# Projections split into chunks and a woven instruction order in a one-core Mamba, attention and feed-forward kernel

## What is computed

```
x = x + layernorm(mamba(layernorm(x)))
x = x + layernorm(two_layers(layernorm(x)))

mamba:   xb, z = split(x @ in_proj);  xb = silu(conv4(xb) + conv_b)
         dt = softplus(...); state = exp(dt * a) * state + dt * b * xb; y = sum(state * c)
         out = ((y + D * xb) * silu(z)) @ out_proj
layer:   q, k, v = split(shift(x) @ wqkv); q, k normalised and rotated; o = local_attention(q, k, v)
         x = x + o @ wo
         a, g = split(layernorm(shift(x)) @ w1 + b1);  x = x + (a * gelu(g)) @ w2 + b2
```

## Time and profile before

| | |
|---|---|
| time, median of 3 runs | 2461.28 us (2460.6 to 2464.99) |
| time of the profiled execution | 2461.61 us |
| its span, first to last instruction | 2459.8 us |
| mean granted clock of TensorE | 0.943 of full speed |
| instructions | 44075 |

### The profile page before, as it was taken

One profiled execution on the slowest core, in us unless ns is written; L12 is line 12 of the kernel. 1 busy time (PEld: TensorE's weight loads), 2 busy tenths in 40 slices (PEclk: granted clock), 3 DMA queues, 4 the chain that ended last, 5 costly groups with the idle time before them and its releaser, 6 DMA issues.

```text
span 2459.8 us, 44075 instructions
## 1 busy us (share of the span) xinstructions
PE 1893.9 (77%) x15808; PEld 1114.3 (45%) x15936; DVE 1892.7 (77%) x3477; ACT 1778.1 (72%) x3955; POOL 1711.4 (70%) x1540
## 2 busy tenths in 40 slices
PE   2156778797878879797878879697888879787865
PEld 0013345353635445363635445363645545363634
DVE  3557797978879797988878797988879797887442
ACT  2245778696978878696878878696877869685644
POOL 1969595977959596886959596885959597792010
PEclk9977999899999989999999999999999989999988
DMA  4444443535344343534544353534543353531000
GB/s 162 126 120 115 112 105 104 132 83 146 103 130 117 100 121 92 134 86 131 129 129 103 103 124 96 138 87 130 130 115 99 110 127 90 137 99 33 17 20 9
DMA packets 126346, 261.09 MB, mean 106 GB/s; under 512 B 26928, under 2 KB 59696, under 8 KB 125872
## 3 DMA queue, kind: packets, MB, share of 16 engines
q1 hardware_dynamic: 126128, 258.27, 39.6%
HBM read 185.42 MB, written 42.99 MB: 93 GB/s over the span
## 4 chain that ended last, share of the span: by engine, by line
PE 38%; DVE 23%; ACT 13%; issue 9%; POOL 8%; DMA 4%; SPq 0%; DVEq 0%; POOLq 0%; ACTq 0%
DVE hs L618 6%; DVE m L892 4%; PE f_bank L342 4%; PE b_bank L342 4%; DVE kr L906 3%; POOL gy L663 3%; DMA spread<-steps 3%; POOL dbu L646 3%; ACT da L594 3%; PE b_bank L703 3%; PE f_bank L746 3%; PE y_sum L571 2%; DVE b_bank L896 2%; PE b_bank L773 2%; DVE ss L879 2%
## 5 line engine op out<-in xcount | busy, mean ns | idle before, releaser
L618 DVE TENSOR_TENSOR_SCAN hs<-da,dbu 128x512 f32<-128x512 f32 x512 | 622.2, 1215 | 127.1 <-POOL dbu L646 82.0
L663 POOL TENSOR_TENSOR gy<-hs,bc 128x512 f32<-128x512 f32 x512 | 652.1, 1274 | 41.5 <-DVE hs L618 31.2
L646 POOL TENSOR_TENSOR dbu<-spread,bc 128x512 f32<-128x512 f32 x512 | 651.5, 1274 | 9.1 <-DMA spread<-steps 9.0
L594 ACT ACTIVATE da<-spread,rest 128x512 f32<-128x512 f32 x512 | 359.4, 702 | 159.0 <-DVE hs L618 135.1
L703 PE MATMUL b_bank<-rest,h_t 128*128 128x512 f32 x384 | 227.9, 694 | 96.6 <-DVE kr L906 92.5
L960 POOL TENSOR_TENSOR kr<-kr,rn 128x512 f32<-128x512 f32 x256 | 264.8, 1043 | 42.3 <-ACT rn L817 37.0
L703 PE MATMUL f_bank<-rest,h_t 128*128 128x512 f32 x384 | 217.6, 665 | 72.1 <-DVE kr L906 64.2
L571 PE MATMUL y_sum<-gy,rest 128*32 128x512 f32 x1024 | 147.0, 649 | 92.4 <-POOL gy L663 92.3
L342 PE MATMUL f_bank<-first,kr 128*128 128x128 f32 x768 | 128.4, 298 | 78.9 <-DVE kr L906 49.8
L342 PE MATMUL b_bank<-first,kr 128*128 128x128 f32 x768 | 123.7, 296 | 57.8 <-DVE kr L906 41.8
L1106 POOL TENSOR_TENSOR xs<-xs,v 128x512 f32<-128x512 f32 x16 | 18.9, 1183 | 213.3 <-ACT xs L337 213.3
(11 more groups left out here) (168 smaller groups left out, 4748.2 us busy)
## 6 DMA issues: line engine op xcount, KB each, us to landing
spread<-steps SPq DMA_DIRECT2D x256, 512.0 KB, 5.1
vs<-v SPq DMA_DIRECT2D x96, 260.0 KB, 5.9
bc<-bc_rows SPq DMA_DIRECT2D x32, 512.0 KB, 6.2
steps<-k_t SPq DMA_DIRECT2D x32, 512.0 KB, 2.7
gate<-gates SPq DMA_DIRECT2D x32, 512.0 KB, 5.7
gates<-kr SPq DMA_DIRECT2D x16, 512.0 KB, 3.4
gates<-late SPq DMA_DIRECT2D x16, 512.0 KB, 4.3
vs<-v SPq DMA_DIRECT2D x32, 130.0 KB, 4.5
```

The source lines that it names most:

```text
L594: e.activation(da[:, :], spread[:, slot(b, s // 2), 0, :], ACT.Exp, scale=a_neg[:, s:s + 1]).then_inc(decayed.sem, 1)
L618: e.tensor_tensor_scan(hs[:, s % 2, :], da[:, :], dbu[:, s % 2, :], 0.0, ALU.mult, ALU.add).then_inc(scanned.sem, 1)
L646: e.tensor_tensor(dbu[:, s % 2, :], spread[:, slot(b, s // 2), 1, :], bc[:, s % 2, :], ALU.mult).then_inc(fed.sem, 1)
L663: e.tensor_tensor(gy[:, s % 8, :], hs[:, s % 2, :], bc[:, 2 + s % 2, :], ALU.mult).then_inc(read_out.sem, 1)
```

## The change

- **Chunks of wo.** The four turns of o and the wo projection become steps `turn_out(c)` and `project_out(c)`. Turns 0 and 1 go ahead of the last head's values (they need heads 0 to 3 only); the projection runs as one step for each chunk, four matmuls for the four token tiles, accumulating in X[1] instead of O. Turns 0, 2 and 3 go through X[0].
- **Chunks of w2 and of the output projection.** w2 runs as three steps, each behind the gate of its chunk, and the output projection as two. For B, w2 sums into L1 instead of L0 (`f.sum`), and what frees the banks for the next element's takes follows.
- **Tables.** In several ACT steps `use_table` goes ahead of the wait.
- **Weaving.** A letter's stream now runs through all elements; the word is repeated, and a second string says how many steps of each letter are left out at first, in place of `AHEAD`. The one-time table work moves into the first step of M.
- **New words for all five engines.** Most of the order is as before. For one period, with +0 for the element whose position the letter gives, PE and SP read as follows where they differ most:

```diff
-def weave(word, **streams):
+def weave(word, late, **chains):
-    for part in word.split():
-        for _ in range(int(part[1:]) if part[0] in streams else 0):
-            next(streams[part[0]], None)
-    for s in streams.values():
-        for _ in s:
-            pass
+    late = {part[0]: int(part[1:]) for part in late.split()}
+    while chains:
+        for part in word.split():
+            for _ in range(int(part[1:])):
+                if late[part[0]]:
+                    late[part[0]] -= 1
+                elif part[0] in chains and next(chains[part[0]], chains) is chains:
+                    del chains[part[0]]
...
+                self.sum = L0 if w is wf else L1
...
         def act_norm_scale(E, e, w, b):
+            E.use_table(EXP_LN)
             E.wait_ge(*w.measured(b, 1))
-            E.use_table(EXP_LN)
...
-            E.wait_ge(*gated(b, 1))
             E.wait_ge(*scanned(b, NSCAN - 1))
-            for t in range(NT):
-                for h in range(NH2):
-                    op = e.matmul(da[:, t * P:(t + 1) * P], yg[h][:, t * P:(t + 1) * P], w_out[:, h, :], start=h == 0,
-                                  stop=h == 1)
-            op.then_inc(out_projected.sem, 1)
-            yield
+            for h in range(NH2):
+                E.wait_ge(*gated(b, h))
+                for t in range(NT):
+                    op = e.matmul(da[:, t * P:(t + 1) * P], yg[h][:, t * P:(t + 1) * P], w_out[:, h, :],
+                                  start=h == 0 and t == 0, stop=h == 1, skip_group_check=True)
+                if h:
+                    op.then_inc(out_projected.sem, 1)
+                yield
...
-                    E.wait_ge(*(f.gelu_made(b - 1, 2), f.gated(b - 1, 2), f.added(b - 1))[n])
+                    E.wait_ge(*(f.added(b - 1) if bank is f.sum else f.gated(b - 1, 2)))
...
+            def turn_out(c):
+                E.wait_ge(*w.o_done(b, 2 * c + 1))
+                if c < 2:
+                    E.wait_ge(*w.p_copied(b, HEADS - 2 + c))
+                else:
+                    E.wait_ge(*w.o_copied(b, 0 if c == 2 else 2))
+                pe_turn(e, X[c == 1], lambda n: w.o[:, n, c * P:(c + 1) * P]).then_inc(w.o_turned.sem, 1)
+
+            def project_out(c):
+                E.wait_ge(*w.o_copied(b, c))
+                if c == 0:
+                    E.wait_ge(*w.o_copied(b, 1))
+                for t in range(NT):
+                    op = e.matmul(X[1][:, t * P:(t + 1) * P], w.o_t[:, c, t * P:(t + 1) * P], wo[:, l, c, :],
+                                  start=c == 0 and t == 0, stop=c == NC - 1, skip_group_check=True)
+                return op
...
+                else:
+                    for c in range(2):
+                        turn_out(c)
+                        yield
                 value(2 * g + 1)
                 yield
...
+            turn_out(2)
+            yield
+            for c in range(2):
+                project_out(c)
+                yield
+            turn_out(3)
+            yield
+            project_out(2)
+            yield
+            project_out(3).then_inc(w.wo_done.sem, 1)
             yield
...
-            E.wait_ge(*f.gated(b, 2))
-            for t in range(NT):
-                for c, (c0, n) in enumerate(HCH):
-                    k = P if c == 2 else n
-                    op = e.matmul(L0[:, t * P:(t + 1) * P], f.ff[0:k, c, t * P:(t + 1) * P], w2[0:k, l, c, :], start=c == 0,
-                                  stop=c == 2)
-            op.then_inc(f.out.sem, 1)
-            yield
+            for c, (c0, n) in enumerate(HCH):
+                k = P if c == 2 else n
+                if c == 0:
+                    E.wait_ge(*(f.gated(b, 1) if f is f0 else f.gelu_made(b, 2)))
+                E.wait_ge(*f.gated(b, c))
+                for t in range(NT):
+                    op = e.matmul(f.sum[:, t * P:(t + 1) * P], f.ff[0:k, c, t * P:(t + 1) * P], w2[0:k, l, c, :],
+                                  start=c == 0 and t == 0, stop=c == 2, skip_group_check=True)
+                if c == 2:
+                    op.then_inc(f.out.sem, 1)
+                yield
```

More of the change, by code:

```diff
@@ L587, in act_state @@
             else:
+                act_tables(E, e)
                 E.wait_ge(*a_made(0))
@@ L611, in skip @@
                                        ALU.add).then_inc(skipped.sem, 1)
+            if b == 0:
+                dve_tables(E, e)
             for s in range(NSCAN):
@@ L761, in pe_attention @@
                     yield
+                else:
+                    for c in range(2):
+                        turn_out(c)
+                        yield
                 value(2 * g + 1)
                 yield
-            E.wait_ge(*w.o_done(b, HEADS - 1))
-            for c in range(NC):
-                if c > 1:
-                    E.wait_ge(*w.o_copied(b, c - 2))
-                pe_turn(e, X[c % 2], lambda n: w.o[:, n, c * P:(c + 1) * P]).then_inc(w.o_turned.sem, 1)
-                yield
-            E.wait_ge(*w.o_copied(b, NC - 1))
-            for t in range(NT):
-                for c in range(NC):
-                    op = e.matmul(O[:, t * P:(t + 1) * P], w.o_t[:, c, t * P:(t + 1) * P], wo[:, l, c, :],
-                                  start=c == 0, stop=c == NC - 1)
-            op.then_inc(w.wo_done.sem, 1)
+            turn_out(2)
+            yield
+            for c in range(2):
+                project_out(c)
+                yield
+            turn_out(3)
[3 more added lines that the diff above has]
+            project_out(3).then_inc(w.wo_done.sem, 1)
             yield
@@ L869, in act_attention @@
                 E.wait_ge(*w.o_turned(b, c))
-                e.activation(w.o_t[:, c, :], X[c % 2][:, :], ACT.Copy).then_inc(w.o_copied.sem, 1)
+                e.activation(w.o_t[:, c, :], X[c == 1][:, :], ACT.Copy).then_inc(w.o_copied.sem, 1)
                 yield
@@ L944, in dve_attention @@
             E.wait_ge(*w.wo_done(b))
-            e.tensor_tensor(x[:, :, :], x[:, :, :], tm(O), ALU.add).then_inc(w.x_added.sem, 1)
+            e.tensor_tensor(x[:, :, :], x[:, :, :], tm(X[1]), ALU.add).then_inc(w.x_added.sem, 1)
             yield
@@ L1048, in dve_feed_forward @@
             E.wait_ge(*f.out(b))
-            e.tensor_tensor(x[:, :, :], x[:, :, :], tm(L0), ALU.add).then_inc(f.added.sem, 1)
+            e.tensor_tensor(x[:, :, :], x[:, :, :], tm(f.sum), ALU.add).then_inc(f.added.sem, 1)
             yield
@@ L1156, in act_tables, with program, elements @@
         def act_tables(E, e):
+            E.use_table(EXP_LN)
             E.wait_ge(*rest_loaded(0))
-            E.use_table(EXP_LN)
             e.activation(a_neg[:, :], a_neg[:, :], ACT.Exp).then_inc(a_exp.sem, 1)
-        def program(name, streams, once=None, at=0):
+        def program(name, **streams):
+            def elements(E, e, stream):
+                for b in range(B):
+                    yield from stream(E, e, b)
             def body(e):
                 E = Engine(e)
-                for k in range(-3, B + 1):
-                    if k == at and once:
-                        once(E, e)
-                    weave(ORDER[name], **{letter: stream(E, e, k + AHEAD[letter])
-                                          for letter, stream in streams.items() if 0 <= k + AHEAD[letter] < B})
+                weave(*ORDER[name], **{letter: elements(E, e, stream) for letter, stream in streams.items()})
                 if name == "sp":
@@ L1180, in build @@
         with nc.Block() as block:
[L1181 to L1186 removed]
+            block.sync(program("sp", C=sp_end, B=sp_back, A=sp_front, M=sp_state, F=sp_steps, E=sp_enter, S=sp_spill))
+            block.gpsimd(program("pool", C=pool_end, B=pool_back, A=pool_front, M=pool_state, F=pool_steps))
+            block.scalar(program("act", C=act_end, B=act_back, A=act_front, M=act_state, F=act_steps, E=act_enter))
+            block.vector(program("dve", C=dve_end, B=dve_back, A=dve_front, M=dve_state, E=dve_enter))
+            block.tensor(program("pe", B=pe_back, A=pe_front, M=pe_state, E=pe_enter))
 FIRST = [("ident", (P,)), ("w_in", (2 * DI,)), ("conv_w", (NH2, NCONV)), ("conv_b", (NH2,)), ("w_x", (NH2, 2 * NS + RANK)),
```

29 lines of the change are left out of this document (12 added, 17 removed), and 25 rows, old and new, of the table ORDER.

## The result

| | before | after |
|---|---|---|
| median of 4 runs, us | 2461.48 | 2485.39 |
| lowest to highest, us | 2460.6 to 2464.99 | 2479.61 to 2496.01 |
| ratio to before | 1 | 1.0101, 95% interval 1.0071 to 1.0132 |
| profiled execution, us (span) | 2461.6 (2459.8) | 2479.61 (2477.8) |
| mean granted clock of TensorE | 0.943 | 0.914 |

What follows compares the result with a forecast made beforehand. No engine was busy over 77%, so order and waits set the time. Handover 18 us plus start and end 7 us, other terms 0, made 25 us off 2461.6: 2437 us, own range 2422 to 2450, whole range 2404 to 2472.

Steps and rivals of the forecast that it cites:

- wo in chunks: B's wo projection on PE split into four pieces of 0.96 us; relief and delay for A cancel, taken at 0.
- The handover: Where DVE's q/k rotations give way to POOL's state work: B.K0 earlier on PE saves 1.3 us a period, 18 us.
- POOL's extra normalisation ahead of d0: Start of the state: one more 1.04 us normalisation before d0, covered by DVE's full queue; taken at 0, uncovered 1.0 lost.
- The end of the state: POOL's waits for scans there: taken at 0; bounds up to 1.1 us gained each period and 1 us lost.
- more is gained: Rival, chance 0.20: POOL's waits for scans go (15 us) and half the remaining handover (6 us): 2416, down to 2404 us.
- w2 and output projection in chunks: PE between last y sum and turn of x: chunks save nothing, dt 0.3 us later but hidden; taken at 0, bounds 0 and 1.8.
- Start and end: Two table loads of 1.28 us moved, last element's wo and w2 and A's last element shortened: together 7 us.
- The slower rival: PE between last y sum and E.dt1: up to 3.64 us added against 1.8 slack; 2476, up to 2493 us; chance 0.17.
- SP's order: G5 goes ahead of E's load, which waits for DVE's square sums of B; taken at 0, no loss.
- DVE's wait before B's k2: Sign of being right: DVE's wait before the rotation of B's k2 falls from 1.67 us to about 0.4 or less.
- POOL's at the handover: Sign of being right: POOL's wait before B.q2, 1.77 us for the inverse norms, goes.
- Line 579: Runs once per element; sign of being right: it repeats every 136.9 us on average instead of 138.1.

Runs made afterwards that it cites:

- a_ffmr: Kernel after, the shift (-mean x rs) of stream B's feed-forward normalisation alone done as four one-column instructions with rs as per-partition scalar: 2450.95 us, ratio 0.9953 to before.
- a_mr: Kernel after, the shift of every normalisation done as four one-column instructions with rs as per-partition scalar: 2451.04 us, ratio 0.9962 to before.
- a_ffmr_r: a_ffmr measured again, five rounds beside another variant on one chip: 2445.88 us, ratio 0.9940 to before.
- a_mr_pool: a_mr with POOL's B.q0 put back behind M.d1 instead of ahead of M.d0: 2452.81 us, ratio 0.9968 to before.
- a_cv: Kernel after with its original shift, one convolution step (cv1) put ahead of stream B's feed-forward shift on DVE: 2470.76 us, ratio 1.0038 to before.
- b_fmr: Kernel before, stream B's feed-forward shift moved from behind scan 27 to behind scan 28 on DVE: 2462.03 us, ratio 1.0003 to before.

## Why the prediction was wrong

**The step that failed** is in "wo in chunks": I walked the new order "with the durations of the rows", which held each DVE instruction at what it took before. The shift's duration before, 0.35 to 0.8 us for 0.14 us of work, was already a wait for POOL; it stood in no term, and the order moved it to where the wait is 3.0 us, with POOL's next product waiting for the scan behind it. Price: 27.6 us in the profiled executions, 34 and 40 in the medians. Without it the kernel after takes 2446 to 2451, which is still 9 to 14 us above the forecast: the period is then 139.7 us, where the kernel before had 139.5 and the forecast 1.3 less.

**The handover, 1.3 us in each period, 18 in all, failed as well,** by the bound that its own text gives: "0, if another wait opens". The waits that it named did go. DVE's before the rotation of B's k2 is 0.26 us in a_ffmr, where it was 1.28 (means of elements 1 to 12), and POOL's for the inverse norms fell from 20.7 to 8.6 us in ten periods, 1.2 each. But the waits of DVE for ACT's squares did not shrink in total. Between 700 and 2100 us, before and in a_ffmr:

```profile
DVE m L892 <- ACT sq L796: 30.6, 30, 1.9
```

```profile
DVE m L927 <- ACT sq L831: 55.8, 49, 2.8
```

The largest new one stands at the start of the state. There scan 0 is now behind the rotation of B's k1, and POOL's first `gy` behind scan 0. ACT, DVE and POOL in the kernel after:

```profile
720.70 0.60 ACT L826 ACTIVATE sq<-b_bank 128x512 f32<-128x512 f32 x1 [1.11 <-PE b_bank L714]
721.40 0.69 DVE L922 TENSOR_TENSOR m<-b_bank,tab 128x512 f32<-128x512 f32 x1 [1.58 <-ACT sq L826]
722.01 1.21 DVE L629 TENSOR_TENSOR_SCAN hs<-da,dbu 128x512 f32<-128x512 f32 x1
723.36 1.27 POOL L674 TENSOR_TENSOR gy<-hs,bc 128x512 f32<-128x512 f32 x1 [1.54 <-issue]
```

What is late is the two projections of PE in front, and what makes them late is the clock. PE sits idle for 3.85 us ahead of them (1.80 before) and then runs at a granted clock of 0.50, the level of 1.2 GHz. In two of the elements 2 to 13 of the same execution it ran at 1.00 from the start, and there POOL's first `gy` did not wait at all. One of those two, then one of the others (the columns are those of the earlier trace rows):

```profile
433.81 1.98 PE L714 MATMUL b_bank<-rest,h_t 128*128 128x512 f32 x4 [3.85 <-DVE kr L936]
716.88 3.78 PE L714 MATMUL b_bank<-rest,h_t 128*128 128x512 f32 x4 [3.85 <-DVE kr L936]
```

```profile
433.80:437.30 3.50, 3.50 (x8) 1.57 (x9) 3.50 (x7) 1.33 (x3) 3.50 (x4) 1.00 0.38 87
716.90:720.40 3.50, 3.50 (x4) 1.49 (x5) 2.92 (x5) 0.72 (x2) 3.50 (x4) 0.50 0.24 54
```

The wait goes into the period. In a_mr and a_ffmr_r one element each has none of it, and stage 1 takes 97.5 us there, against 98.5 to 100.0 in the elements of a_mr, a_ffmr and a_ffmr_r that wait 1.5 us or more. So by an estimate from these rows some 1.7 us a period is lost to it, which is more than the 1.3 that was forecast as gain. No run keeps the clock up there, so this is read from elements side by side and not from an edit. POOL also has a new wait at the handover itself, for the last square sum of B, 0.7 to 1.5 us:

```profile
1175.35 0.24 POOL L982 TENSOR_SCALAR ss<-ss 128x16 f32<-128x16 f32 x1 [1.41 <-DVE ss L909]
```

**POOL's extra normalisation ahead of d0, taken at 0.** Right in the sum (a_mr_pool within 2 us of a_mr). Its cover was named as "DVE's full queue", and that is wrong: DVE has the wait of 1.58 us there. The normalisation only changes sides of d0: put back, it made stage 1 1.2 us longer and stage 2 1.0 us shorter. So of the 1.7 us that stage 1 gains in a_ffmr (100.7 to 99.0) some 1.2 is moved work, and 0.5 is gain.

**The end of the state, taken at 0, up to 1.1 as a rival.** The waits for scans behind the first did fall by the size that the rival "more is gained" had, 21.4 to 12.8 us or 0.9 a period, but in the middle of the state and not at its end, and the new wait for scan 0 took 1.5 back.

**w2 and output projection in chunks, taken at 0 with 0.3 us for dt.** Too low. Stage 2 is 1.9 us longer (38.8 to 40.7 in a_ffmr): 0.9 at the y normalisation, 0.3 at dt0 to fin, 0.7 at fin to d0, less 0.1 at x1 to dt0. The 0.7 is the normalisation moved ahead of d0; 1.1 is left for this term. I had looked for the cost of in3 behind B.a2 (0.86 us, measured 0.93) at E.dt1 only, where it didn't fall. It fell one step earlier, on z1, which stands ahead of the y normalisation's logarithm on ACT. With 1.7 gained in stage 1 and 1.9 lost in stage 2, moved work included in both, a_ffmr's period is 139.7 against 139.5.

**Start and end, 7 us.** Right in kind, low in size, and all that a_ffmr gains: the d0 of element 2 comes 3.3 us sooner, and from the start of the last scan to the end it takes 242.8 us for 250.6. From the last division to the addition it is 4.4 us, as these rows of after show, for 8.5 before, where I had counted 6.1 and claimed 1.5 less:

```profile
2445.89 0.42 DVE L961 TENSOR_TENSOR kr<-b_bank,rd 128x256 f32<-128x256 f32 x1
2450.31 0.69 DVE L975 TENSOR_TENSOR xs<-xs,b_bank 128x512 f32<-128x512 f32 x1 [4.00 <-PE b_bank L774]
...
2469.36 0.69 DVE L1082 TENSOR_TENSOR xs<-xs,b_bank 128x512 f32<-128x512 f32 x1 [1.95 <-PE b_bank L1032]
```

**The slower rival, 2476 to 2493,** holds the measured 2485 for another reason. Its place was right in part (in3 behind B.a2) and is worth 6 us, not 25 to 39. SP's order, taken at 0, shows nothing either way: POOL's `dbu` waited 9.0 us for loads of `spread` in the whole execution, before and after.

**What the text named as signs.** DVE's wait before B's k2 (0.25 us in the kernel after) and POOL's at the handover did shrink, as expected. Line 579 (L586 after) repeats every 140.3 us on average, from 140.7 to 2244.8, where 138.1 was before and 136.9 expected:

```profile
L586 PEld LDWEIGHTS da<-rest,y x128: 190/192/337, 140.7 to 2244.8; 128*128 128x128 f32 x128
```

## What to carry to other kernels

An instruction's duration in a profile is not its cost when it is far above that of its shortest instance: 0.14 us of work at a median of 0.57 was a wait, and a wait moves with the order. Before weaving small VectorE instructions between GpSimd products, ask which of them read two tensors of SBUF, and give the second as a per-partition scalar where it can be, one column at a time (one tensor of four columns was held up as well): a few lines of code were worth 34 us here. A wait removed in one place says little until the waits of the same engine are added up over the whole period: DVE's one at B's k2 went, and its total rose from 30.6 to 55.8 us. A step moved ahead in an in-order queue has to be followed to the first consumer it delays (z1 on ACT), not only to the one in question (dt1).

## What the runs showed that I had not expected

- A VectorE instruction held up by GpSimd does not get its turn at the end of the product that runs: in 10 of 14 elements of the kernel after it missed two or three boundaries between back-to-back products (in a_cv mostly one) and took 2.4 to 3.7 us, until GpSimd itself paused. Which of them miss is open. In the kernel after those that began 0.53 to 0.59 us ahead of a boundary missed it, as did one at 0.05, and those at 0.20, 0.76, 1.01 and 1.02 us got through, but in the kernel before and in b_fmr some at 0.55 to 0.57 got through as well.
- Holding the y normalisation up by 0.93 us a period, or freeing it, moved the period by only 0.2 to 0.7 us, in either kernel.
- Within one execution of the kernel after, the same two projections ahead of scan 0 took 1.98 us in two elements and up to 3.78 in the others, behind the same idle time of 3.85 us. Why TensorE's clock fell in the others and not in these two, no row shows.
